# An AdaLN block with a Mamba-2 scan on one core: the first stage moved into the main block, wide modulation products, a polynomial log1p, C stored once

## The chip, the cores and the metric

The kernel runs on one core of a Trainium2 chip. The metric is the device time of one execution in microseconds, the median of several. All data is float32. Matmuls whose operands are typed float32r take one record in the profile, those on plain float32 take two.

## What is computed

The reference, cut to what matters here (4 batches of 512 tokens, width 512; 64 value heads of 16, 8 groups of 64 states, chunks of 64 in this kernel):

```python
mod = (silu(c) @ wmod).reshape(4, 6, 1, -1)           # (4,512) @ (512,3072)
sa, ca, ga, sb, cb, gb = (mod[:, i] for i in range(6))
h = layernorm(x) * (1 + ca) + sa
xBCzA = einsum('bld,ed->ble', h, in_proj_w)           # x 1024, B 512, C 512, z 1024, A_log 64
xBC = silu(conv1d(xBC, taps=4) + bias)
dt = softplus(A_log)                                  # log1p(exp(-|a|)) + max(a, 0)
y = ssd_chunk_scan(x, -dt, B, C) + D * x / dt         # per head
x = x + ga * ((y * silu(z + z_bias)) @ out_proj_w.T)
h = layernorm(x) * (1 + cb) + sb
x = x + gb * (h @ binarize(ffn_w).T + bias)
```

The scan per group and chunk: G = B C^T (gram); M = G times exp of differences of summed dt (mix); y = M x (diagonal) + exp(sums) * C S (offdiagonal); S = decay * S + B^T (w x) (fade, states, update).

## The kernel before

There are three parts: `prologue`, a block of its own that ends in a barrier over all engines; `main_part`; and `tail_part` (output projection and second half), which the change touches only in the names of PSUM banks.

`prologue` makes, in this order on each engine: the modulation (`section(0)` and `section(1)`: transposed products with 4 columns, 16 matmuls a section); statistics and normalisation of the 16 x tiles, their transposition (`turn`), `h_hi` and `h_lo` (`make_h`, `low_part`), four tiles of 128x512 a batch; `dt_inputs` for the two pairs of batches (`pb` 0 and 1), 24 matmuls each; two more sections; the weights of the first six tiles (`weights`); the two gate sections in the wide form (4x512 outputs). Meanwhile DVE computes dt for both pairs, interleaved: log1p by a series of atanh (21 operations a pair, two reciprocals among them), the summed dt, their ends, low parts, skips D/dt. All goes to scratch in DRAM; the main block reads it back, among it the negated sums (`na_scratch`).

`main_part` works in 16 steps (4 group pairs by 4 batches), each with 4 units of 128 tokens; 64 units in all, each of four slots. A fixed table (`tile_order`) says which half projection (6 matmuls of 512 columns) stands in which slot, a lag table when its linear part, taps, tanh and silu follow. The first four tiles (x, x, B, C of step 0) are projected ahead of the loop. In unit v's slot 0 PE runs `offdiagonal(v)` (L1039), `states(v+1)` (L1052), `diagonal(v)` (L1065), `gram(v+1)` (L1077); `turn_x` (L1019), `turn_b` (L1029) and `decay` (L1010) of unit v+2 stand in slots 1 to 3. DVE runs `update`, `collect` and `mix` (L1277) in slots 1 and 2, convolutions (L1241) and silus (L1263, L1268) between. C is stored as a block diagonal of two 64-row halves, the rest zero, so that full 128-row matmuls give both groups at once.

## Time and profile before

| | |
|---|---|
| median of 3 runs | 749.23 us (749.15 to 751.7) |
| profiled execution | 748.24 us |
| its span, first to last instruction | 746.5 us |
| mean granted PE clock | 0.944 of full speed |
| PE, DVE, ACT, POOL busy | 674.1, 536.5, 376.5, 389.4 us |

A row of the timeline reads: start, duration, engine, line, operation, output <- inputs, shape, count; in brackets the idle time before it and what ended it. Ends of matmuls are modelled, so the distance between starts is what counts on PE.

### The profile page before, as it was taken

The numbers are of one execution on the slowest core, as the hardware profiler recorded it, in microseconds if no ns is written. First come the engines' busy times: TensorE is split into PE (matmuls) and PEld (weight loads), VectorE is DVE, ScalarE is ACT, GpSimd is POOL, SyncE is SP. The second block draws the span as 40 slices with busy tenths as digits, with TensorE's granted clock in tenths as the row PEclk, the third lists the DMA queues.
The fourth block names the chain that finished last, engine by engine and source line by source line (L and its number), as shares of the span: only waits on it lengthen the run. The fifth ranks groups of instructions, "written<-read, shape, count | busy, mean of one in ns | idle before, by whom it ended". The sixth has DMA issues, their size and how long they took to land. (4 is left out here: it accounts for less than half of the span.)

```text
span 746.5 us, 20781 instructions
## 1 busy us (share of the span) xinstructions
PE 674.1 (90%) x8194; PEld 527.1 (71%) x8194; DVE 536.5 (72%) x940; ACT 376.5 (50%) x812; POOL 389.4 (52%) x465
## 2 busy tenths in 40 slices
PE   6679256899999999999999999999998999999995
PEld 6458115677777777787777777777776777777783
DVE  2768675878788688778777777877779567576754
ACT  1563241444564554465454456555665534555453
POOL 3674920125365454375363365454645767677771
PEclk9757577999999999999999999999999999999997
DMA  8450262103132112222212225223212664443401
GB/s 207 107 177 12 80 247 90 32 16 110 37 104 84 58 61 72 82 92 61 92 58 69 70 80 152 91 68 114 77 48 70 202 191 134 141 136 112 128 28 43
DMA packets 61908, 71.54 MB, mean 96 GB/s; under 512 B 13992, under 2 KB 32936, under 8 KB 61812
## 3 DMA queue, kind: packets, MB, share of 16 engines
q1 hardware_dynamic: 56372, 70.17, 29.6%
q8 instruction: 65, 1.06, 0.6%
q10 hardware_dynamic: 5440, 0.05, 0.4%
q14 instruction: 31, 0.25, 0.1%
HBM read 54.45 MB, written 15.75 MB: 94 GB/s over the span
## 5 line engine op out<-in xcount | busy, mean ns | idle before, releaser
L1241 DVE SCALAR_TENSOR_TENSOR m_cv<-bank,gpc,m_cv 128x511 f32<-128x511 f32 (+2 forms) x192 | 143.5, 748 | 44.9 <-ACT m_cv L1151 40.3
L1001 PE MATMUL bank<-h_hi,w_hi 128*128 128x512 f32 x384 | 159.0, 414 | 12.8 <-DVE m_Xp L1323 11.5
L1001 PE MATMUL bank<-h_hi,w_lo 128*128 128x512 f32 x384 | 151.8, 395 | 0.0
L1001 PE MATMUL bank<-h_lo,w_hi 128*128 128x512 f32 x384 | 151.5, 394 | 0.0
L1151 ACT ACTIVATE m_cv<-bank,gpc 128x512 f32<-128x512 f32 x96 | 71.9, 748 | 92.0 <-PE bank L1001 92.0
L1379 POOL TENSOR_TENSOR m_S<-m_S,m_cd 128x128 f32<-128x128 f32 x96 | 39.7, 414 | 141.0 <-DVE m_S L1304 71.4
L1001 PEld LDWEIGHTS bank<-h_hi,w_hi 128*128 128x128 f32 x384 | 73.0, 190 | 31.9 <-DVE m_Xp L1323 11.7
L1370 POOL TENSOR_TENSOR m_Xw<-m_Xp,wend 128x256 f32<-128x256 f32 x64 | 39.8, 622 | 105.8 <-ACT m_Xp L1171 105.8
L1001 PEld LDWEIGHTS bank<-h_hi,w_lo 128*128 128x128 f32 x384 | 72.6, 189 | 17.1
L1001 PEld LDWEIGHTS bank<-h_lo,w_hi 128*128 128x128 f32 x384 | 73.1, 190 | 13.7
L1163 ACT ACTIVATE m_M<-bank 128x512 f32<-128x512 f32 x128 | 76.2, 595 | 12.0 <-PE bank L1010 10.5
L1277 DVE TENSOR_TENSOR m_M<-m_M,bank 128x512 f32<-128x512 f32 x128 | 81.7, 679 | 0.0
L1065 PE MATMUL pair<-m_M,m_Xp 64*32 64x64 f32 x4096 | 61.6, 227 | 0.0
L1010 PE MATMUL bank<-R,Lm 84*128 84x512 f32 x128 | 57.2, 447 | 3.2 <-ACT m_M L1163 3.2
L1158 ACT ACTIVATE bank<-m_cv 128x512 f32<-128x512 f32 x96 | 58.2, 606 | 2.6 <-DVE m_cv L1241 2.6
L1707 PE MATMUL bank<-h_hi,t_y_hi 128*128 128x512 f32 x128 | 52.1, 407 | 7.0 <-POOL t_y_lo L1584 7.0
L1065 PEld LDWEIGHTS pair<-m_M,m_Xp 64*32 64x32 f32 x4096 | 54.0, 106 | 1.1
L1584 POOL TENSOR_TENSOR t_y_lo<-h_lo_place,t_y_hi 128x1024 fp32r<-128x1024 f32 x16 | 40.1, 2504 | 27.3 <-ACT t_y_hi L1545 27.3
L1707 PE MATMUL bank<-h_hi,t_y_lo 128*128 128x512 f32 x128 | 50.7, 396 | 0.0
L1707 PE MATMUL bank<-h_lo,t_y_hi 128*128 128x512 f32 x128 | 50.7, 396 | 0.0
L1268 DVE SCALAR_TENSOR_TENSOR m_gate<-bank,m_cv 128x512 f32<-128x512 f32 x32 | 22.1, 691 | 39.3 <-ACT bank L1158 39.3
L1171 ACT ACTIVATE m_Xp<-bank 128x256 f32<-128x256 f32 x64 | 24.2, 379 | 49.0 <-PE bank L1019 49.0
(183 smaller groups left out, 1376.3 us busy)
## 6 DMA issues: line engine op xcount, KB each, us to landing
m_ea<-ea_scratch SPq DMA_DIRECT2D x32, 256.0 KB
m_dd<-dd_scratch SPq DMA_DIRECT2D x32, 256.0 KB
y_scratch<-m_t SPq DMA_DIRECT2D x16, 512.0 KB, 3.4
h_lo_place<-y_scratch SPq DMA_DIRECT2D x16, 512.0 KB, 4.3
p_wm<-in_L_wmod_dram SPq DMA_DIRECT2D x6, 1024.0 KB, 6.4
m_wraw<-in_L_attn_in_proj_w_dram SPq DMA_DIRECT2D x18, 256.0 KB, 2.9
p_xt<-in_L_attn_input__dram SPq DMA_DIRECT2D x16, 256.0 KB, 3.0
w_lo_place<-in_L_attn_input__dram SPq DMA_DIRECT2D x16, 256.0 KB, 4.5
```

The source lines that it names most:

```text
L1001: ins = pe.matmul(A[k % 3][:, :], w[:, t, kc, :], h[:, n % NB, kc, :], start=(m == 0), stop=(m == 11))
L1010: pe.matmul(DB[:, :], s.Lm[:, u % 2, q, :], s.R[:, u % 2, q, :], start=True, stop=True).then_inc(d_done, 1)
L1065: ins = pe.matmul(YS[32 * j:32 * j + 32, c, q * Q:(q + 1) * Q], Xp[half, u % 2, HG * q + h, :], M[half, u % 2, q, h * Q:(h + 1) * Q], star ...
L1151: act.activation(cv[:, k % 3, :], A[k % 3][:, :], ACT.Identity, scale=scale, bias=bias).then_inc(lin_done, 1)
L1158: act.activation(A[k % 3][:, :], cv[:, k % 3, :], ACT.Tanh).then_inc(tanh_done, 1)
L1163: act.activation(M[:, u % 2, q, :], DB[:, :], ACT.Exp).then_inc(exp_done, 1)
L1241: ins = dve.scalar_tensor_tensor(out=cv[:, k % 3, lag:], in0=A[k % 3][:, 0:L - lag], scalar=s.gpc[:, gp, o:o + 1], in1=cv[:, k % 3, lag:], ...
L1277: dve.tensor_tensor(m, m, g, ALU.mult).then_inc(m_done, 1)
L1370: pool.tensor_tensor(Xw[:, :, :].rearrange("p q (j e d) -> p (q j) e d", e=2, d=HD), src, w, ALU.mult).then_inc(xw_done, 1)
L1379: pool.tensor_tensor(S1[:, c, :].rearrange("p (h d) -> p h d", h=HG), S[:, (m - 1) % 4, :].rearrange("p (h d) -> p h d", h=HG), cd[:, gp, ...
L1584: pool.tensor_tensor(y_lo[:, st.b % 2, :, :], yt_v(st.b), y_hi[:, st.b % 2, :, :].bitcast(F32), ALU.subtract).then_inc(ylo_done, 1)
L1707: ins = pe.matmul(OB[i][:, :], y[:, i, k, :], w[k], start=(k == 0 and m == 0), stop=(k == KI - 1 and m == 2))
```

## The change

The prologue is no longer a block of its own: `first_part` defines functions that the main block's engines call ahead of their loops, so the barrier goes. The x tiles are loaded before the modulation weights. All six sections are wide products (4 matmuls with 512 columns), copied to SBUF and turned back by four small transposes. dt of batches 0 and 1 (`pb` 0) is computed early; x tiles 12 to 15, the projections of the first four tiles, and the inputs of dt of batches 2 and 3 follow. Of `pb` 1, `softplus` and `finish_times` stand ahead of DVE's loop, `sums`, `low_sums` and `skips` inside it (units -1, 1, 3), the decays on ACT in unit 1, the turn of the end decays in unit 4, their copies in unit 5; the stores and the chunk decays of `pb` 1 in SP's units 2 and 5. log1p is a polynomial of degree 11. The negated copies in scratch are gone (the constant is -1 instead). C is stored once, `[P, 2, L]`, and `offdiagonal`, `states` and `gram` use 64x64 tiles; gram's product moves to PSUM beside the others (`YS[:, q, 384:448]`), which brings waits on `g_done` for `collect` and `update`, and `offdiagonal` waits for `m_done` in place of `turn_b`.

```diff
+LOG1P = [1.0, -0.5, 0.33333237, -0.2499676, 0.19956708, -0.16365153, 0.13033364, -0.09139414, 0.04930997, -0.01718427,
+         0.00280164]
...
-            for k in (15, 13, 11, 9, 7, 5, 3):
-                for pb in range(2):
-                    r, e, den, sv, tt, pl, dt, tmp = half_of(pb)
-                    linked(pb)
-                    link(pb, dve.scalar_tensor_tensor(out=pl, in0=pl, scalar=1.0 / k, in1=tt, op0=ALU.add, op1=ALU.mult))
...
+        sp.dma_start(c4[:, :], cond).then_inc(d_c, 16)
+        for i in range(4):
+            load_x(i)
+        sp.dma_start(wa_raw[:, :], w_in[2 * DI + 2 * NG * NS:, :]).then_inc(d_wa, 16)
+        load_section(0)
+        load_section(1)
+        for i in range(4, 8):
+            load_x(i)
+        load_weights(0)
+        load_weights(1)
+        for i in range(8, 12):
+            load_x(i)
+        load_weights(2)
+        load_weights(3)
+        load_section(2)
+        load_section(3)
+        for i in range(12, 16):
+            load_x(i)
+        load_weights(4)
+        load_weights(5)
+        load_section(4)
+        load_section(5)
...
+        normalize(10)
+        normalize(11)
+        softplus(dve, 0)
+        finish_times(dve, 0)
+        sums(dve, 0)
+        skips(dve, 0)
+        low_sums(dve, 0)
...
+        normalize(15)
+        low_part(9)
+        low_part(11)
+        convolve(0)
+        convolve(1)
+        silu(0)
+        low_part(13)
+        low_part(15)
+        convolve(2)
+        silu(1)
+        convolve(3)
+        silu(2)
+        silu(3)
+        modulation(2)
+        modulation(3)
+        gates()
+        softplus(dve, 1)
+        finish_times(dve, 1)
...
+    def softplus(dve, pb):
+        e, pl = s.chain[:, pb, 1, :], s.chain[:, pb, 3, :]
+        dve.wait_ge(a_exp[pb], 3)
+        dve.tensor_scalar(pl, e, LOG1P[-1], None, ALU.mult).then_inc(a_v[pb], 1)
+        for i, c in enumerate(LOG1P[-2:4:-1]):
+            chained(dve, pb, 1 + i)
+            dve.scalar_tensor_tensor(out=pl, in0=pl, scalar=c, in1=e, op0=ALU.add, op1=ALU.mult).then_inc(a_v[pb], 1)
+    def finish_times(dve, pb):
+        dt, e, pl = (s.chain[:, pb, i, :] for i in (0, 1, 3))
+        for i, c in enumerate(LOG1P[4::-1]):
+            chained(dve, pb, 6 + i)
+            dve.scalar_tensor_tensor(out=pl, in0=pl, scalar=c, in1=e, op0=ALU.add, op1=ALU.mult).then_inc(a_v[pb], 1)
+        chained(dve, pb, 11)
+        dve.tensor_tensor(dt, pl, dt, ALU.add).then_inc(a_v[pb], 1)
+        chained(dve, pb, 12)
+        dve.tensor_scalar(e, dt, DT_MAX, -1.0, ALU.min, ALU.mult).then_inc(a_v[pb], 1)
+    def sums(dve, pb):
+        end, pl = s.chain[:, pb, 1, :], s.chain[:, pb, 3, :]
+        plv = pl.rearrange("p (c q) -> p c q", q=Q)
+        dve.wait_ge(konst, 16)
+        chained(dve, pb, A_DT)
+        dve.tensor_tensor_scan(out=pl, data0=chunk_on[:, :], data1=end, initial=0.0,
+                               op0=ALU.mult, op1=ALU.add).then_inc(a_v[pb], 1)
+        chained(dve, pb, A_SUM)
+        dve.tensor_tensor(end.rearrange("p (c q) -> p c q", q=Q), plv[:, :, Q - 1:Q].broadcast_to([P, NC, Q]), plv,
+                          ALU.subtract).then_inc(a_v[pb], 1)
+    def low_sums(dve, pb):
+        hi, pl = s.chain[:, pb, 2, :], s.chain[:, pb, 3, :]
+        dve.wait_ge(a_act[pb], B_CD)
+        dve.tensor_tensor(pl, pl, hi, ALU.subtract).then_inc(a_v[pb], 1)
+    def skips(dve, pb):
+        dt = s.chain[:, pb, 0, :]
+        dve.reciprocal(dt, dt).then_inc(a_skip, 1)
+        dve.wait_ge(a_skip, 2 * pb + 1)
+        dve.tensor_scalar(dt, dt, dcol[:, 0:1], None, ALU.mult).then_inc(a_skip, 1)
...
+    def decays(act, pb):
+        end, hi, pl, ea = (s.chain[:, pb, i, :] for i in (1, 2, 3, 4))
+        act.wait_ge(a_v[pb], A_END)
+        act.activation(hi.bitcast(F32R), pl, ACT.Copy).then_inc(a_act[pb], 1)
+        act.activation(ea, pl, ACT.Exp).then_inc(a_act[pb], 1)
+        act.activation(cde[:, pb, :], pl.rearrange("p (c q) -> p c q", q=Q)[:, :, Q - 1], ACT.Exp).then_inc(a_act[pb], 1)
+        act.activation(end, end, ACT.Exp).then_inc(a_act[pb], 1)
...
-                for m in range(KC):
-                    for k in range(KC):
-                        ins = pe.matmul(MOD[n // 2][:, (n * KC + m) * NB:(n * KC + m + 1) * NB],
-                                        wm[:, n % 2, k, m * P:(m + 1) * P], scT[:, k, :],
-                                        start=(k == 0), stop=(k == KC - 1))
-                ins.then_inc(mod_pe, 1)
...
+            for k in range(KC):
+                ins = pe.matmul(row_bank(n)[0:NB, :], scT[:, k, :], wm[:, n % 2, k, :], start=(k == 0), stop=(k == KC - 1))
+            ins.then_inc(sec_pe, 1)
...
+        def turn_section(n):
+            pe.wait_ge(sec_cp, n + 1)
+            for k in range(KC):
+                ins = pe.transpose(mod_bank(n)[:, k * NB:(k + 1) * NB], row_of(n)[:, k * P:(k + 1) * P], s.ident[0:NB, 0:NB])
+            ins.then_inc(mod_pe, 1)
...
+        for i in range(4, 8):
+            turn(i)
+        for n in range(4):
+            weights(n)
+        pe.wait_ge(wa_dve, 1)
+        dt_inputs(0)
+        pe.wait_ge(w_act, 4)
+        for i in range(8, 12):
+            turn(i)
+        for n in range(4, 8):
+            weights(n)
+        project(0, 0)
+        project(0, 1)
+        section(2)
+        section(3)
+        project(1, 0)
+        project(1, 1)
+        turn_section(2)
+        turn_section(3)
+        for i in range(12, 16):
+            turn(i)
+        project(2, 0)
+        project(2, 1)
+        for n in range(8, 12):
+            weights(n)
+        project(3, 0)
+        project(3, 1)
+        section(4)
+        section(5)
+        pe.wait_ge(w_act, 12)
+        end_turn(pe, 0)
+        turn_section(4)
+        turn_section(5)
+        dt_inputs(1)
+        pe.wait_ge(gate_v, 3)
+        pe.transpose(MOD[0:2 * NB * KC, 0:P], ga[:, :, :, :].rearrange("p g b k -> p (g b k)"), s.ident[:, :]).then_inc(gate_pe, 1)
+        pe.wait_ge(gate_ready, 1)
+        pe.wait_ge(a_exp[1], 2)
...
+                if v == -1:
+                    start.store_skips(sp, 0)
+                    for i2 in range(2):
+                        sp.wait_ge(start.h_lo[i2], 8)
+                    load_skips(0)
+                if v == 2:
+                    start.store_decays(sp, 1)
+                    load_chunk_decays(1)
+                if v == 5:
+                    start.store_skips(sp, 1)
+                if v == 4 or (v > 2 and i == 2 and n < LAST):
+                    load_skips(v // UPS + (v != 4))
...
-                wait(pe, m_done, 2 * u)
                 wait(pe, bt_read, u)
-                pe.transpose(GB[:, P:2 * P], Bt[:, n % 2, tok(u)], s.ident[:, :]).then_inc(bt_done, 1)
+                pe.transpose(GB[:, 0:P], Bt[:, n % 2, tok(u)], s.ident[:, :]).then_inc(bt_done, 1)
             def offdiagonal(u):
                 n = u // UPS
                 wait(pe, y1_done, u)
                 pe.wait_ge(s_new, n_new(u, 1))
+                pe.wait_ge(m_done, 2 * u + 2)
...
-                    ins = pe.matmul(YS[:, c, P:2 * P], S[:, (2 * u + c - 1) % 4, :], Ct[:, n % 2, :, chunk(u, c)],
-                                    start=True, stop=True)
+                    for j in range(2):
+                        for q in range(2):
+                            group, strip = slice(64 * q, 64 * q + 64), slice(64 * j, 64 * j + 64)
+                            ins = pe.matmul(YS[strip, q, P + Q * c:P + Q * c + Q], S[group, (2 * u + c - 1) % 4, strip],
+                                            Ct[group, n % 2, chunk(u, c)], start=True, stop=True)
...
-                for m in range(4):
+                for q in range(2):
                     for c in range(2 if u % UPS < UPS - 1 else 1):
-                        half = slice(64 * c, 64 * c + 64)
-                        ins = pe.matmul(YS[32 * m:32 * m + 32, c, 256:384], BTs[half, 32 * m:32 * m + 32], Xw[half, m // 2, :],
-                                        start=True, stop=True)
+                        half, group = slice(64 * c, 64 * c + 64), slice(64 * q, 64 * q + 64)
+                        ins = pe.matmul(YS[group, c, 256:384], BTs[half, group], Xw[half, q, :], start=True, stop=True)
...
-                for m in range(4):
-                    first = (u % UPS) * U_TOK + 32 * m
-                    ins = pe.matmul(GB[32 * m:32 * m + 32, 0:P], Bt[:, n % 2, first:first + 32], Ct[:, n % 2, :, chunk(u, m // 2)],
-                                    start=True, stop=True)
+                for c in range(2):
+                    for q in range(2):
+                        group = slice(64 * q, 64 * q + 64)
+                        ins = pe.matmul(YS[64 * c:64 * c + 64, q, 384:384 + Q], Bt[group, n % 2, chunk(u, c)],
+                                        Ct[group, n % 2, chunk(u, c)], start=True, stop=True)
...
-            pe.wait_ge(zeroed, 1)
-            for k in range(4):
-                project(k, 0)
-                project(k, 1)
+            start.tensor(pe, project)
...
+                    if (v, sl) == (4, 3):
+                        pe.wait_ge(xp_done, u + 1)
+                        start.end_turn(pe, 1)
...
+                    if (v, sl) == (1, 1):
+                        start.decays(act, 1)
+                    if (v, sl) == (5, 0):
+                        start.end_copy(act, 1)
...
-                if t == 3:
-                    for q in range(2):
-                        rows = slice(64 * q, 64 * q + 64)
-                        ins = dve.scalar_tensor_tensor(out=Ct[rows, n % 2, q, :], in0=A[k % 3][rows, :], scalar=1.0,
-                                                       in1=cv[rows, k % 3, :], op0=ALU.add, op1=ALU.mult)
-                    ins.then_inc(silu_done, 1)
-                    return
...
-                g = GB[:, q * Q:(q + 1) * Q].unsqueeze(1).broadcast_to([P, HG, Q])
+                g = YS[:, q, 384:384 + Q].unsqueeze(1).broadcast_to([P, HG, Q])
...
+                dve.wait_ge(g_done, min(u + 2, NU))
...
+                dve.wait_ge(g_done, u + 1)
...
-            dve.memset(Ct[:, :, :, :], 0.0)
-            dve.memset(Xp[:, :, :, :], 0.0).then_inc(zeroed, 1)
-            dve.wait_ge(zeroed, 1)
-            convolve(0)
-            convolve(1)
-            silu(0)
-            convolve(2)
-            silu(1)
-            convolve(3)
-            silu(2)
-            silu(3)
+            start.vector(dve, convolve, silu)
...
+                    if (v, sl) == (-1, 3):
+                        start.sums(dve, 1)
+                    if (v, sl) == (1, 3):
+                        start.low_sums(dve, 1)
+                    if (v, sl) == (3, 3):
+                        start.skips(dve, 1)
```

Where instructions move. First PE in unit 0 of the loop, from the turn of B of unit 2 to the gram of unit 1, before:

```order
L1029 MATMUL bank<-ident,m_Bt 128x128 [waits m_bt_read,m_m_done]
L1039 MATMUL pair<-m_Ct,m_S 128x128 [waits m_s_new]
L1052 MATMUL pair<-m_Xw,m_BTs 32x128 [waits m_bt_read,m_xw_done,m_s_new]
L1052 MATMUL pair<-m_Xw,m_BTs 32x128 x7
L1065 MATMUL pair<-m_M,m_Xp 32x64 [waits m_xp_done,m_m_done]
L1065 MATMUL pair<-m_M,m_Xp 32x64 x31
L1077 MATMUL bank<-m_Ct,m_Bt 32x128 [waits m_bt_read]
L1077 MATMUL bank<-m_Ct,m_Bt 32x128 x3
```

The same place after the change:

```order
L1176 MATMUL bank<-ident,m_Bt 128x128 [waits m_bt_read]
L1190 MATMUL pair<-m_Ct,m_S 64x64 [waits m_m_done,m_s_new]
L1190 MATMUL pair<-m_Ct,m_S 64x64 x3
L1203 MATMUL pair<-m_Xw,m_BTs 64x128 [waits m_bt_read,m_xw_done,m_s_new]
L1203 MATMUL pair<-m_Xw,m_BTs 64x128 x3
L1215 MATMUL pair<-m_M,m_Xp 32x64 [waits m_xp_done,m_m_done]
L1215 MATMUL pair<-m_M,m_Xp 32x64 x31
L1228 MATMUL pair<-m_Ct,m_Bt 64x64 [waits m_bt_read]
L1228 MATMUL pair<-m_Ct,m_Bt 64x64 x3
```

One matmul of 128 columns became four of 64 (two became eight in the other units), eight became four, and the wait on `m_m_done` moved from the turn to the first of them. Second, DVE around the first taps of the loop itself; before, from C's silus of step 0:

```order
L1263 SCALAR_TENSOR_TENSOR m_Ct<-bank,m_cv 64x512 [waits m_tanh_done]
L1263 SCALAR_TENSOR_TENSOR m_Ct<-bank,m_cv 64x512
L1241 SCALAR_TENSOR_TENSOR m_cv<-bank,gpc,m_cv 128x511 [waits m_lin_done]
L1241 SCALAR_TENSOR_TENSOR m_cv<-bank,gpc,m_cv 128x510 [waits m_tap_done]
L1241 SCALAR_TENSOR_TENSOR m_cv<-bank,gpc,m_cv 128x509 [waits m_tap_done]
L1304 COPY m_S<-pair 128x128 [waits m_st_done]
```

After, from C's one silu of step 0 (`chain` holds dt and its sums):

```order
L1414 SCALAR_TENSOR_TENSOR m_Ct<-bank,m_cv 128x512 [waits m_tanh_done]
L461 TENSOR_SCALAR mod_t<-pair 128x16 [waits p_mod_pe] x2
L482 TENSOR_SCALAR p_gs<-pair 128x32 [waits p_gate_abs]
L483 TENSOR_SCALAR p_ga<-p_ga 128x32
L485 SCALAR_TENSOR_TENSOR p_ga<-p_gs,p_ga 128x32 [waits p_gate_v]
L559 TENSOR_SCALAR chain<-chain 128x512 [waits p_a_exp1]
L562 SCALAR_TENSOR_TENSOR chain<-chain 128x512 [waits p_a_v1] x5
L569 SCALAR_TENSOR_TENSOR chain<-chain 128x512 [waits p_a_v1] x5
L571 TENSOR_TENSOR chain<-chain 128x512 [waits p_a_v1]
L573 TENSOR_SCALAR chain<-chain 128x512 [waits p_a_v1]
L1393 SCALAR_TENSOR_TENSOR m_cv<-bank,gpc,m_cv 128x511 [waits m_lin_done]
```

The gates and the second pair's dt now stand between the first four tiles and the loop's first taps.

## Rows read from the trace of the kernel before

**Rows 1.** The page: busy time, and the clock in 40 slices (tenths).

```profile
PE 674.1 (90%) x8194; PEld 527.1 (71%) x8194; DVE 536.5 (72%) x940; ACT 376.5 (50%) x812; POOL 389.4 (52%) x465
...
PEclk9757577999999999999999999999999999999997
```

**Rows 2.** Timeline, 0 to 50 us: modulation products, statistics, h, dt inputs.

```profile
6.78 13.79 PE L653 MATMUL pair<-p_scT,p_wm 128*128 128x4 f32 x64 [2.36 <-DMA p_wm<-in_L_wmod_dram]
7.37 0.69 DVE L408 BATCH_NORM_STATS2 p_st<-p_xt 128x6 f32<-128x512 f32 x1 [2.73 <-DMA p_xt<-in_L_attn_input__dram]
...
25.39 0.78 ACT L575 ACTIVATE h_hi<-bank,mod_t 128x512 fp32r<-128x512 f32 x1 [3.72 <-PE bank L670]
...
30.04 0.81 ACT L579 ACTIVATE p_hf<-bank,mod_t 128x512 f32<-128x512 f32 x1
...
33.41 0.78 ACT L575 ACTIVATE h_hi<-bank,mod_t 128x512 fp32r<-128x512 f32 x1 [2.56 <-PE pair L670]
...
49.19 0.78 PE L684 MATMUL bank<-h_hi,p_wa_hi 128*128 128x512 f32 x1
```

**Rows 3.** Timeline, 54 to 100 us: the dt series, GpSimd beside it, wide sections.

```profile
56.54 0.69 DVE L466 TENSOR_SCALAR p_a<-bank 128x512 f32<-128x512 f32 x1 [0.52 <-PE bank L684]
...
73.11 11.12 POOL L378 TENSOR_TENSOR w_lo<-p_wst,w_hi 128x256 fp32r<-128x256 f32 x1 [9.83 <-ACT p_wst L616]
...
74.61 4.90 DVE L488 SCALAR_TENSOR_TENSOR p_a<-p_a 128x512 f32<-128x512 f32 x8
...
82.50 2.81 DVE L506 TENSOR_TENSOR_SCAN p_a<-p_chunk_on,p_a 128x512 f32<-128x512 f32 x2
...
85.24 2.28 DVE L514 TENSOR_TENSOR p_a<-p_a 128x512 f32<-128x512 f32 x2
...
91.17 1.41 POOL L378 TENSOR_TENSOR w_lo<-p_wst,w_hi 128x256 fp32r<-128x256 f32 x2 [0.30 <-ACT p_wst L616]
...
94.97 9.62 PE L728 MATMUL bank<-p_wm,p_scT 128*4 128x512 f32 x16 [1.65 <-DMA p_wm<-in_L_wmod_dram]
...
97.47 3.35 DVE L526 RECIPROCAL p_a<-p_a 128x512 f32<-128x512 f32 x1
```

**Rows 4.** Busy us of PE, PEld, DVE, ACT, POOL in a window; PEclk; DMA share; GB/s.

```profile
75.00:80.00 5.00, 0.00 (x0) 0.00 (x0) 5.00 (x9) 0.00 (x0) 5.00 (x1) 0.50 0.21 52
...
295.00:323.00 28.00, 27.95 (x453) 22.14 (x452) 21.50 (x41) 14.46 (x32) 11.07 (x16) 1.00 0.23 73
```

**Rows 5.** Timeline where the main block begins: first projection, turn_x(0), taps of tile 4.

```profile
117.11 0.80 PE L1001 MATMUL bank<-h_hi,w_hi 128*128 128x512 f32 x1 [11.50 <-DVE m_Xp L1323]
...
132.66 0.38 PE L1019 MATMUL bank<-ident,m_xs 128*128 128x128 f32 x2
...
136.68 2.32 DVE L1241 SCALAR_TENSOR_TENSOR m_cv<-bank,gpc,m_cv 128x511 f32<-128x511 f32 x3
```

**Rows 6.** Timeline of PE, slot 0 of two units of the loop.

```profile
318.32 0.39 PE L1039 MATMUL pair<-m_Ct,m_S 128*128 128x128 f32 x2
318.73 0.45 PE L1052 MATMUL pair<-m_Xw,m_BTs 64*32 64x128 f32 x16
...
325.59 0.61 PE L1039 MATMUL pair<-m_Ct,m_S 128*128 128x128 f32 x4
326.21 0.45 PE L1052 MATMUL pair<-m_Xw,m_BTs 64*32 64x128 f32 x16
326.44 0.91 PE L1065 MATMUL pair<-m_M,m_Xp 64*32 64x64 f32 x64
327.28 0.43 PE L1077 MATMUL bank<-m_Ct,m_Bt 128*32 128x128 f32 x8
327.64 0.44 PE L1094 MATMUL bank<-ident,m_wraw 128*128 128x128 f32 x2
```

**Rows 7.** The last turn_x on PE; then from the waits, 150 to 630 us: total, times, longest.

```profile
593.42 0.38 PE L1019 MATMUL bank<-ident,m_xs 128*128 128x128 f32 x2
...
PEld bank L1029 <- DVE m_M L1277: 2.7, 6, 1.9
```

974 lines of the change are left out of this document (488 added, 486 removed).

## The prediction

> **What bounds the kernel now.** I read the page first, then its 40 slices, then the timeline of the first 140 us, then two units of the main loop. The page [rows 1] shows TensorE (PE) busy for 90% of the span and no other engine over 72%. Its clock row stands under 9 from the second to the seventh slice, up to 131 us, and not again before the last one: there PE runs with gaps and for long stretches at half clock. So there are two regimes, and the change touches both.
>
> In the main loop PE is the bound. In a window of 28 us [rows 4] PE is busy for 27.95 and DVE for 21.50, so DVE has 6.5 us free, about 1.7 us a unit. Unit 0 turns its x at 132.66 [rows 5] and unit 63, the last of 64, at 593.42 [rows 7]: 460.8 us for 63 units, 7.31 us each.
>
> The first stage is a chain over all engines. PE is busy for 0.00 us between 75 and 80 [rows 4] while DVE works through the softplus series. In turn: the modulation products end at 20.57 and the first normalised tile of h is made at 25.39 [rows 2]; h is made batch by batch, the inputs of dt start on PE at 49.19; DVE's chain for all four batches follows, and only then does a barrier let the first projection begin, at 117.11, after 11.50 us in which PE waited for the zeroing of Xp on DVE [rows 5]. The first convolution that belongs to the loop itself (tile 4) starts on DVE at 136.68 [rows 5]. I take that row as the anchor: behind it both kernels have the same list of work on DVE, but for what the change moves there.
>
> **The first stage, step by step.** The changed one is laid out by hand, each engine in its order, with durations of before.
>
> (a) The x tiles are loaded ahead of the wide weights, so statistics can start at about 4.5 instead of 7.37 [rows 2]. The modulation takes 8 records of 512 columns a section instead of 32 of 4 columns. Before, two sections took 13.79 us for 64 records [rows 2]. The gates were already made in the wide form, 16 records in 9.62 us, 0.60 each [rows 3], partly at half clock. At full clock I estimate 0.42 (four times the 0.105 of a 128-column record, below): 3.4 a section. The weights land later, behind 1.1 MB of x; I put section 0 at 9.3, two turns of 0.65 between, section 1 up to 17.4, a copy, four small turns and the additions 2 us: h from 19.5, not 25.39.
>
> (b) A batch of h takes ACT 5.46 us (25.39 to 30.85 [rows 2]). Batches followed each other every 8.0 us (25.39 to 33.41), which DVE and GpSimd set with the statistics: the next one from 28, until 33.5. With its last low part 35, then the dt inputs of batches 0 and 1: 24 matmuls, 7.3 us before (49.19 to the first DVE reader at 56.54 [rows 2, 3]): 43. Three activations: 45.
>
> (c) DVE's chain for these two: the series was 21 operations for each pair of batches, two of them reciprocals of 3.35; now it is 18 with one. A link is 4.90 / 8 = 0.61 with two chains interleaved [rows 3]; alone I take 0.70. 11 x 0.70 + 1.4 (scan) + 1.14 (end) + 3.35 + four lesser ones at 0.5 = 15.6: 61. Meanwhile GpSimd is held up: its low part of the weights took 11.12 us beside DVE's links and 0.70 where DVE was idle [rows 3]. Its four weight pieces, for which ACT waits and with ACT the exponentials of the decays, end about 60: 63 for DVE.
>
> (d) Tiles 12 to 15 are normalised: 75. h of batch 3 on ACT: 81. DVE works off four low parts, twelve taps and four silus meanwhile; PE projections 2 and 3, with weights between: 88.
>
> (e) PE then has in a row sections 4 and 5 (6.9), small turns (1.5) and the dt inputs of batches 2 and 3 (6 to 7): 103; softplus inputs 105. DVE: 11 x 0.70 and two lesser ones, 8.7: 113.7. For stretches at half clock, which bursts after a gap had before, I add 2.4: **the anchor comes at 116, 20.7 us earlier**. PE, which would be ready for unit 0 at 107, 25 earlier, waits for DVE in the first units.
>
> (f) What went into the loop: for batches 2 and 3 scan, ends, low sums and skips, 1.4 + 1.14 + 3.35 and two lesser ones, 7 us on DVE (units -1, 1 and 3), 2.9 us of activations on ACT, four turns on PE. It lies beside 1.7 us a unit of free DVE time, 13 us over eight units; where that cover is gone it costs 7. As the backlog of (e) uses the same cover, I charge **2.0**. SP's queue: the stores of batches 2 and 3 stand behind the loads for units 4 to 6, whose data is wanted two units later; nothing.
>
> **The loop, per unit.** Removed: one of two DVE silus of C in four units, off the bound. On PE [rows 6]: L1039 is 0.41 to the next row with two records and 0.62 with four, so 0.105 a record and 0.20 fixed, the emptying of the array before the next tile shape. L1052, L1065 and L1077 are 0.23, 0.84 and 0.36, that is 13.1 ns a record in L1065; L1077 as two rounds of 0.105 with 0.15 fixed. With L1039's mean (half a unit fewer in four) the three that change cost 1.16 a unit.
>
> After, they are 14, 7 and 8 records on 64x64 tiles, and the order of shapes gives one more change between full and split array. No row has this tile. Lower bound: a record of 64 columns goes at 13.1 ns whatever its width, one of 128 columns in a quarter of 0.105: 0.18 + 0.18 + 0.10, and three emptyings of 0.15 = 0.91, so -0.25 a unit. Upper bound: 13.1 ns is the load of 32 columns and 64 take 26.2: 0.37 + 0.18 + 0.21 and 0.45 = 1.21, +0.05. The rows can't separate them (every split row loads 32 columns). I choose -0.05, nearer the upper one, since 64 columns load twice of what L1065 loads. **62 x -0.05 = -3.**
>
> "TensorE: Matmul & The Clock Gate", section LDWEIGHTS, of the Trainium skill says that a weight load's time goes by the number of columns alone; "TensorEngine Tiling (Array Packing)", Key Properties, of the Trainium skill says that a change of tiling mode drains the array. By both the loop would lose its 0.05 a unit, 3 us, and the time would be 733.
>
> The wait for C's product moves: it is no longer turn_b that waits for M's last product but L1039 one row later, so nothing is added. New is that DVE's update and collect wait for gram, about 0.36 after the diagonal; behind them stands M's product, for which PE waited in about 6 of 62 units, 2.7 us in all [rows 7].
>
> **Sum.** The profiled execution took 748.24, its span 746.5, the median is 749.23. 748.24 - 20.7 + 2.0 - 3.1 = 726.4; with the median's 1 us more, 727.
>
> **Rivals.**
> - *As forecast*, first stage 14 to 27 earlier, loop within 0.1 a unit: 716 to 736. 0.52.
> - *64x64 tiles pay*: -0.25 to -0.35 a unit (the longer if turn_b's missing wait and L1039's fixed part go too), 15 to 22 us and the first stage at its best: 703 to 716. For it: half of C's columns were zeros. 0.22.
> - *Loads by columns, with another emptying of the array*: 0.05 to 0.2 a unit, 3 to 12: 733 to 742. 0.10.
> - *The first stage hardly gains*: GpSimd held up by both series, and PE at half clock in six short bursts (each up to 3.4 more): 8 us earlier instead of 20.7: 740 to 745. 0.07.
> - *Slower*: DVE's round becomes the loop. Update and collect start 0.36 later and the additional emptying adds 0.15, and if M's product is then always late, a unit takes 0.5 more: 31 us, less 20: 757. It decides from 0.4 a unit (25 us). For it: the 6 late products. Against: 6.5 us in 28 free on DVE. 0.06.
> - The rest, under 703: 0.03.
>
> **Numbers.** 727; range 703 to 742 leaves out the last two and part of the fourth. 0.5% is 3.7 us, about what a measurement of this kernel can tell from no change: faster 0.90, same 0.04, slower 0.06.
>
> **What would show it.** First h_hi at 19 to 21; dt inputs at 35; DVE's first chain ending near 63; sections 4 and 5 near 88 to 95; the tile-4 convolution at 112 to 120; the turn of unit 63 about 24 us earlier; spacing of units 7.2 to 7.35; L1190 with four instructions a chunk 0.4 to 0.55 to the next row. I am wrong if the second series holds up PE for over 8 us in units -2 to 2, if the unit's spacing leaves 7.0 to 7.4, or if PE waits for M's product in most units.

## The result, and the profile after

The changed kernel takes **722.11 us** in the median of 4 runs (720.19 to 725.2), the kernel before beside it 749.76: a ratio of **0.9631**, 95% interval 0.9591 to 0.9671, 27 us less. The forecast was 727, the range 703 to 742. The profiled execution of after took 725.2 us, 3 above its median.

From the page of the changed kernel:

```profile
PE 660.5 (91%) x8347; PEld 497.3 (69%) x8347; DVE 516.7 (71%) x913; ACT 379.1 (52%) x818; POOL 374.9 (52%) x464
...
PEclk9678899999999999999999999999999999999995
```

It answers to [rows 1]: TensorE is still the bound, with fewer busy microseconds, and its clock row is back at 9 after the fifth slice (90 us), not after the seventh (131 us). The 9 of the first slice says little: this trace has no clock level for the first 15.07 us, and the views count such time as full. I come back to this at the narrow sections.

The timeline of the first stage, selected rows of PE, ACT and DVE in order of time:

```profile
11.65 5.28 PE L739 MATMUL bank<-p_wm,p_scT 128*4 128x512 f32 x8 [0.19 <-DMA p_wm<-in_L_wmod_dram]
17.89 3.60 PE L739 MATMUL bank<-p_wm,p_scT 128*4 128x512 f32 x8
22.90 0.78 ACT L643 ACTIVATE h_hi<-bank,mod_t 128x512 fp32r<-128x512 f32 x1 [0.79 <-DVE mod_t L461]
48.44 0.43 DVE L559 TENSOR_SCALAR chain<-chain 128x512 f32<-128x512 f32 x1 [0.27 <-ACT chain L655]
48.90 4.54 DVE L562 SCALAR_TENSOR_TENSOR chain<-chain 128x512 f32<-128x512 f32 x5
53.48 6.27 DVE L569 SCALAR_TENSOR_TENSOR chain<-chain 128x512 f32<-128x512 f32 x5
66.69 0.68 DVE L591 TENSOR_TENSOR chain<-chain 128x512 f32<-128x512 f32 x1
87.91 7.03 PE L739 MATMUL bank<-p_wm,p_scT 128*4 128x512 f32 x16
103.84 0.43 DVE L559 TENSOR_SCALAR chain<-chain 128x512 f32<-128x512 f32 x1 [5.35 <-ACT chain L655]
104.71 0.38 PE L1167 MATMUL bank<-ident,m_xs 128*128 128x128 f32 x2
113.00 2.31 DVE L1393 SCALAR_TENSOR_TENSOR m_cv<-bank,gpc,m_cv 128x511 f32<-128x511 f32 x3
117.45 0.80 PE L1158 MATMUL bank<-R,Lm 84*128 84x512 f32 x1 [4.61 <-ACT m_M L1316]
```

The first h starts at 22.90 (25.39 in [rows 2]); the turn of unit 0 on PE at 104.71 (132.66 in [rows 5]), 28.0 earlier; but the taps of tile 4, my anchor, at 113.00 (136.68 in [rows 5]), 23.7 earlier. The last five rows show why: DVE works off the second softplus series from 103.84 to 113.0, the taps stand behind it, ACT's tanh behind the taps, and PE idles 4.61 us.

A second stall, on DVE and PE five units later:

```profile
149.25 3.34 DVE L596 RECIPROCAL chain<-chain 128x512 f32<-128x512 f32 x1
...
157.00 0.47 PE L1149 MATMUL bank<-h_hi,w_hi 128*128 128x512 f32 x1 [1.68 <-DVE m_xs L1414]
```

From one turn of x to the next the first units take 7.1 to 7.2 us (units 0 to 1: 6.15), but 13.54 between units 1 and 2 and 9.21 between 6 and 7. Unit 8 turns at 169.42 (190.84 before), 21.4 earlier; unit 63 at 570.63 (593.42 in [rows 7]), 22.8 earlier. So the whole loop behind unit 8 gave 1.4 us in 55 units.

Two units of the loop on PE (left out: projections, decay products):

```profile
318.43 0.27 PE L1176 MATMUL bank<-ident,m_Bt 128*128 128x128 f32 x1
318.54 0.38 PE L1245 MATMUL bank<-ident,m_wraw 128*128 128x128 f32 x2
318.85 0.46 PE L1190 MATMUL pair<-m_Ct,m_S 64*64 64x64 f32 x16
319.16 0.45 PE L1203 MATMUL pair<-m_Xw,m_BTs 64*64 64x128 f32 x8
319.54 0.86 PE L1215 MATMUL pair<-m_M,m_Xp 64*32 64x64 f32 x64
320.32 0.34 PE L1228 MATMUL pair<-m_Ct,m_Bt 64*64 64x64 f32 x8
320.60 0.44 PE L1245 MATMUL bank<-ident,m_wraw 128*128 128x128 f32 x2
...
325.78 0.28 PE L1176 MATMUL bank<-ident,m_Bt 128*128 128x128 f32 x1
325.99 0.34 PE L1190 MATMUL pair<-m_Ct,m_S 64*64 64x64 f32 x8
326.52 0.45 PE L1203 MATMUL pair<-m_Xw,m_BTs 64*64 64x128 f32 x8 [0.18 <-ACT m_BTs L1329]
```

Read starts, not durations. From the off-diagonal product (L1190) to the states (L1203) it is 0.31 with 16 records and 0.53 with 8. What decides is the row ahead of it, not the count: over 150 to 560 us it is 0.31 behind a piece of weights and 0.53 behind the turn of B, with 8 and with 16 records alike. From the turn of B (L1176) to the states it is 0.73 and 0.74. I come back to this.

### The profile page after: what moved, and what is told of

Same layout as the page of the kernel before. It is cut to its first block and busy times, and to the rows that moved or that the text cites. A ratio compares the mean times of both kernels' runs of the same rounds, so it can differ in the third digit from the quotient of the medians.

```text
span 723.5 us, 21285 instructions
## 1 busy us (share of the span) xinstructions
PE 660.5 (91%) x8347; PEld 497.3 (69%) x8347; DVE 516.7 (71%) x913; ACT 379.1 (52%) x818; POOL 374.9 (52%) x464
## 5 line engine op out<-in xcount | busy, mean ns | idle before, releaser
L1149 PE MATMUL bank<-h_hi,w_hi 128*128 128x512 f32 x384 | 161.0, 419 | 4.8 <-ACT p_hf L647 1.7
L1149 PE MATMUL bank<-h_hi,w_lo 128*128 128x512 f32 x384 | 153.9, 401 | 0.0
L1149 PE MATMUL bank<-h_lo,w_hi 128*128 128x512 f32 x384 | 153.4, 400 | 0.0
L1149 PEld LDWEIGHTS bank<-h_hi,w_hi 128*128 128x128 f32 x384 | 74.4, 194 | 20.7 <-issue 6.8
L1423 DVE TENSOR_TENSOR m_M<-m_M,pair 128x512 f32<-128x512 f32 x128 | 81.7, 678 | 0.2 <-issue 0.2
L1215 PE MATMUL pair<-m_M,m_Xp 64*32 64x64 f32 x4096 | 55.4, 224 | 0.0
L1734 POOL TENSOR_TENSOR t_y_lo<-h_lo_place,t_y_hi 128x1024 fp32r<-128x1024 f32 x16 | 39.6, 2474 | 27.8 <-ACT t_y_hi L1695 27.8
L1215 PEld LDWEIGHTS pair<-m_M,m_Xp 64*32 64x32 f32 x4096 | 45.0, 105 | 10.9 <-issue 10.9
```

What stands on the lines that cost most here:

```text
L1149: ins = pe.matmul(A[k % 3][:, :], w[:, t, kc, :], h[:, n % NB, kc, :], start=(m == 0), stop=(m == 11))
L1215: ins = pe.matmul(YS[32 * j:32 * j + 32, c, q * Q:(q + 1) * Q], Xp[half, u % 2, HG * q + h, :], M[half, u % 2, q, h * Q:(h + 1) * Q], star ...
L1423: dve.tensor_tensor(m, m, g, ALU.mult).then_inc(m_done, 1)
L1734: pool.tensor_tensor(y_lo[:, st.b % 2, :, :], yt_v(st.b), y_hi[:, st.b % 2, :, :].bitcast(F32), ALU.subtract).then_inc(ylo_done, 1)
```

## The experiments

The changed kernel came out at 0.9631 and, in a second measurement, at 0.9663 of the kernel before; 0.965 is the yardstick below, and a thousandth is 0.75 us. Single traces of one and the same kernel differ by up to 3.4 us in when the first stage ends, so within a trace I read distances.

**The form of C alone.** The kernel before, with offdiagonal, states, gram, the silu of C and their waits as in the changed one:

```
-                    ins = pe.matmul(YS[:, c, P:2 * P], S[:, ...], Ct[:, n % 2, :, chunk(u, c)], ...)
+                    for j in range(2):
+                        for q in range(2):
+                            ins = pe.matmul(YS[strip, q, ...], S[group, ..., strip], Ct[group, n % 2, chunk(u, c)], ...)
```

> The kernel before, with only the form of C changed: C kept once, its products on 64x64 tiles, states on 64x64 tiles, gram written beside them, the waits that go with it. The zeroing of C's storage stays, so the first stage is untouched. My reading of the trace after (14 + 7 + 8 records cost 1.98 us a unit against 2.05 before, loop spacing 0.025 shorter) gives 62 x -0.025 = -1.6 us: ratio 0.996 to 1.000. If 64x64 tiles paid as the rival had it (-0.25 a unit), 733 to 735, ratio 0.98. If loads by columns and another emptying decided (+0.05), 752, ratio 1.004.

Measured: 746.16 us (12 runs) beside 747.72, ratio 0.9993 (0.9972 to 1.0014); a unit takes 7.234 us (mean of units 12 to 43) where 7.268 was. From the turn of unit 0 to that of unit 63 the two traces differ by 2.0 us (458.8 in place of 460.8), as much as I had expected; in the time the interval reaches from 2 us less to 1 us more. The form of C is worth nothing that the time can show; the rival "64x64 tiles pay" and the one that had them cost 3 to 12 us both fall.

**Gram first.** One group moved:

```
                             states(v + 1)
+                            gram(v + 1)
                         if v >= 0:
                             diagonal(v)
-                        if 0 <= v + 1 < NU:
-                            gram(v + 1)
```

> The changed kernel, with gram issued between states and diagonal: the three products on 64x64 tiles then follow one another and a unit has one change of tile shape fewer (3 in place of 4). If each change costs an emptying of about 0.15 us, and the small products save nothing because of them, a unit takes 0.10 to 0.15 less, 6 to 9 us over 62 units: ratio to the changed kernel 0.988 to 0.992, ratio to the kernel before 0.951 to 0.956. If the change of shape costs nothing and the loads of 64 columns are what eats the gain, nothing: 722, ratio to before 0.963. If DVE's round were close to the bound, gram earlier gives M's product an earlier start and a gain too, but then PE's waits would go and not the spacing of rows in the group.

Measured: 714.47 us, ratio 0.9545 (0.9522 to 0.9568), 8 us less than the changed kernel. The rows of gram_first for the same place in the loop:

```profile
315.67 0.45 PE L1203 MATMUL pair<-m_Xw,m_BTs 64*64 64x128 f32 x8
315.91 0.32 PE L1228 MATMUL pair<-m_Ct,m_Bt 64*64 64x64 f32 x8
316.17 0.86 PE L1215 MATMUL pair<-m_M,m_Xp 64*32 64x64 f32 x64
316.95 0.44 PE L1245 MATMUL bank<-ident,m_wraw 128*128 128x128 f32 x2
```

States and gram took 0.38 + 0.28 = 0.66 us to their next rows; now 0.24 + 0.26 = 0.50. Same records, same shapes, one change from 64x64 to 64x32 tiles and back less: 0.16 us. A unit takes 7.101 in place of 7.256, 0.155 less, and waits of PE are as before. So a change of shape is the price, not the load of 64 columns. What gram's move would give with the old form of C was not tested.

**The second series spread over the loop.** Its 13 links are issued by a table of places behind the taps, the sums a unit or two later:

```
+SERIES_AT = {(-2, 3): 2, (-1, 0): 1, (-1, 1): 1, (-1, 2): 1, (-1, 3): 2, (0, 1): 1, (0, 3): 2, (1, 1): 3}
-        softplus(dve, 1)
-        finish_times(dve, 1)
```

> The changed kernel, with the second softplus series (13 links, 9.2 us on DVE) taken out from ahead of the loop and spread over units -2 to 1 behind the taps, sums, low sums, the decays on ACT and their stores one unit or two later. If the 4.6 us wait of PE in unit 0 (turn to turn 13.54 us where 7.2 is usual) is that series standing ahead of tile 4's taps, the turn of unit 2 comes 4 to 6 us earlier against the first h, and the time falls by 3 to 5: 717 to 719, ratio to before 0.956 to 0.960. If DVE has not 1.7 us a unit free there, the stall only moves to later units and the time stays within 1 us of 722.

Measured: 721.91 us, ratio 0.9647 (0.9621 to 0.9673): nothing that can be told. The wait of 4.61 is gone (unit 2 follows unit 1 by 7.19), but unit 3 takes 11.06, unit 5 8.39, unit 7 9.18, and units 0 to 8 take 64.2 us where they took 64.7. Windows of series_spread (columns: busy time of each engine, then PE's clock):

```profile
core 0: us, PE busy (x) PEld busy (x) DVE busy (x) ACT busy (x) POOL busy (x), PEclk, DMA share, GB/s
103.00:110.00 7.00, 6.54 (x43) 5.16 (x44) 2.60 (x5) 3.31 (x7) 0.62 (x1) 1.00 0.02 5
110.00:117.00 7.00, 6.82 (x112) 5.13 (x111) 6.49 (x12) 3.33 (x7) 1.71 (x3) 1.00 0.13 44
117.00:124.00 7.00, 4.30 (x21) 3.22 (x20) 6.86 (x15) 3.26 (x6) 1.40 (x3) 1.00 0.44 152
```

From 110 to 124 DVE is busy for 6.5 and 6.9 of 7 us; in the changed kernel, without the series in the loop, it is 6.9 from 120 to 127 and 6.1 in the next window. My "1.7 us a unit of free DVE time" is true of a unit in the middle of the loop [rows 4], not of the first ones. The stall is DVE's list, wherever its parts stand. What is free is DVE's time ahead of the loop's work: it is busy for 2.60 of 7 us in the first window.

**The last reciprocal in four pieces.**

```
+SKIP_AT = {(2, 3): 0, (3, 1): 1, (3, 3): 2, (4, 1): 3}
+        dt = s.chain[:, 1, 0, i * P:(i + 1) * P]
+        dve.reciprocal(dt, dt).then_inc(a_skip, 1)
```

> The changed kernel, with the reciprocal of 512 columns of the second skips (3.34 us on DVE in unit 3) cut into four of 128 columns in units 2 to 4. If that one long instruction is what PE waits 1.68 us for in unit 5 (spacing 9.21 in place of 7.2), the spacing there falls to 7.2 to 7.4 and the time by 1.8 to 2.1: 720, ratio to before 0.960. If DVE is simply full in these units, the wait stays wherever the work is put: 722.

Measured: 721.57 us, ratio 0.9642 (0.962 to 0.9664). The stall is gone in the trace (unit 7 follows unit 6 by 7.26, units 0 to 8 take 62.9 in place of 64.7), 1.8 us; the total can't tell 1.8 us from nothing. Here the length of one instruction was the cause and not the sum of the work.

**The changed kernel again.**

> The changed kernel unaltered, as the yardstick for the others on this chip: ratio to before 0.961 to 0.966, first turn at 103 to 105, unit 2 at 13.3 to 13.7 us behind unit 1, unit 7 at 9.2 behind unit 6.

Measured: ratio 0.9663 (0.9639 to 0.9687); spacings 13.85 and 9.19. Its first turn came at 101.33, 3.4 earlier than in the trace above. Its first loads had landed earlier (first h at 21.35, 1.6 earlier); the rest arose on the way.

**The dt inputs of batches 2 and 3 first.** On PE ahead of sections 4 and 5, with ACT and DVE to match:

```
+        dt_inputs(1)
         section(4)
         section(5)
...
-        dt_inputs(1)
```

> The changed kernel, with the dt inputs of batches 2 and 3 on PE ahead of the wide sections 4 and 5 (which only the gates need), the last tanh and the softplus inputs ahead of their copies on ACT, and DVE's second series begun before the gates' additions and finished behind them. The work is the same. In the changed kernel DVE idles 5.1 us before C's silu and 5.35 us before the second series, then PE idles 4.61 us for it; in series_spread the stall moved into later units because DVE was busy 6.8 of 7 us there. If that is the cause, the series put into DVE's earlier idle time takes the stall away for good: taps of tile 4 at 106 to 108 in place of 113.0, unit 2 within 8 us of unit 1, time 4 to 5.5 us less than the unaltered one: 715 to 717, ratio to before 0.956 to 0.958. If the stall is DVE's backlog of the loop itself (taps and silus of tiles 4 to 6), at most 1 us is won.

Measured: 716.31 us, ratio 0.9571 (0.9551 to 0.9591), some 6 us less. DVE in dt_first:

```profile
93.64 0.43 DVE L559 TENSOR_SCALAR chain<-chain 128x512 f32<-128x512 f32 x1 [2.73 <-ACT chain L655]
...
100.94 3.60 DVE L569 SCALAR_TENSOR_TENSOR chain<-chain 128x512 f32<-128x512 f32 x5
...
107.66 2.32 DVE L1393 SCALAR_TENSOR_TENSOR m_cv<-bank,gpc,m_cv 128x511 f32<-128x511 f32 x3 [1.64 <-ACT m_cv L1304]
```

The series starts 10 us earlier, in idle time, and the taps 5.3 us earlier, now with DVE waiting for them; unit 2 follows unit 1 by 7.18. With series_spread this shows the cause of the first stall: work of DVE left for the loop's beginning that had room before it.

**Statistics and small loads early.** The twelve small loads go from ACT's queue to the sync queue, DVE's statistics of tiles 4 to 6 ahead of the modulation's additions.

```
+        statistics(dve, 4)
+        statistics(dve, 5)
+        normalize(4)
+        statistics(dve, 6)
+        normalize(5)
         modulation(0)
         modulation(1)
```

> The changed kernel, with the twelve small vector loads on the sync queue behind the first weights in place of ahead of ACT's copy of the dt weights, and DVE's statistics of x tiles 4 to 6 ahead of the modulation's additions. In the changed kernel ACT idles 15.9 us while these loads are issued, DVE idles 7.06 behind it, and batch 1 of h starts at 32.59 where ACT had finished batch 0 at 28.4. If DVE's late start is what sets batch 1, it starts at 28.5 to 29.5, the first series ends 3 to 4 us earlier (63 in place of 66.7), and the first turn comes 2 to 4 us earlier; time 718 to 720. The first h_hi itself should stay at 22.5 to 22.9, since PE's second section (ends at 21.49) sets it. If PE's own list from the first projection on (sections, projections, turns) sets the end of the first stage, nothing of it is left at the first turn.

Measured: 720.32 us, ratio 0.9617 (0.96 to 0.9634). ACT and DVE no longer idle where they did, but batch 1 of h comes only 0.9 us earlier behind batch 0:

```profile
22.56 1.26 POOL L403 TENSOR_TENSOR h_lo<-p_hf,h_hi 128x512 fp32r<-128x512 f32 x1 [4.45 <-ACT p_hf L647]
23.79 0.22 POOL L411 TENSOR_SCALAR p_rstd<-p_mv 128x1 f32<-128x1 f32 x1
...
29.82 0.78 ACT L643 ACTIVATE h_hi<-bank,mod_t 128x512 fp32r<-128x512 f32 x1 [3.32 <-PE bank L758]
```

The root of tile 6 (23.79) stands in GpSimd's order behind low part 0, which waits for ACT. From the first h to the scan of the first series it is 37.2 us, where it is 37.9 to 38.2 in five traces with this stretch unaltered and 39.3 in two more. A fault of my edit, mended in the last kernel; what it gives by itself lies between 1 and 3 us.

**The polynomial alone**, in the kernel before:

```
-                    link(pb, dve.reciprocal(tmp, den))
+            for c in LOG1P[-2::-1]:
+                    link(pb, dve.scalar_tensor_tensor(out=pl, in0=pl, scalar=c, in1=e, op0=ALU.add, op1=ALU.mult))
```

> The kernel before, with only the softplus series changed: the polynomial in place of the series with a quotient, for both pairs of batches. 28 operations of which two reciprocals of 3.35 us become 24 without one, 7.8 us less on DVE in the stretch in which PE is idle. If DVE's series is on the path to the first projection, the first turn comes 7 to 8 us earlier and the time is 740 (ratio 0.989 to 0.991), so over a quarter of the first stage's gain is the polynomial's and the rest the order's. If GpSimd's low parts or the loads end last there, 0 to 3 us.

Measured: 745.03 us, ratio 0.9949 (0.9936 to 0.9963), about half of what I expected; first turn 2.1 us earlier. Three rows of poly_alone say where it went:

```profile
62.70 0.69 DVE L468 TENSOR_SCALAR p_a<-bank 128x512 f32<-128x512 f32 x1 [3.15 <-PE bank L667]
...
92.99 9.54 PE L711 MATMUL bank<-p_wm,p_scT 128*4 128x512 f32 x16 [3.40 <-DMA p_wm<-in_L_wmod_dram]
...
115.08 0.80 PE L984 MATMUL bank<-h_hi,w_hi 128*128 128x512 f32 x1 [11.51 <-DVE m_Xp L1306]
```

The first reciprocal had lain beside PE's second dt inputs, for which DVE now waits 3.15 us, so the scan comes 3.5 us earlier (82.50 in [rows 3]) and not 7.8; then the gates' weights arrive late, and the first projection is 2.0 earlier (117.11 in [rows 5]).

**The first projections last.** Four projections, their activations, taps and silus stand behind the whole first stage, as behind the barrier before:

```
         pe.wait_ge(a_exp[1], 2)
+        for k in range(4):
+            project(k, 0)
+            project(k, 1)
```

> The changed kernel, with the overlap of the first projections undone: projections 0 to 3, their activations, taps and silus stand behind the whole first stage (behind the second series on DVE), as the barrier had them in the kernel before; everything else, the order of the rest included, is as changed. If the gain came from PE and DVE working beside the first stage, the work put back behind it is 4 projections on PE (2.8 us each) and 12 taps and 4 silus on DVE (about 12 us): the first turn comes 11 to 13 us later, but DVE's series starts up to 10 us earlier, so the taps of tile 4 come 4 to 10 us later than 113.0 and the time is 726 to 732, ratio to before 0.969 to 0.977; most of the 28 us would then be the order within the first stage. If the overlap is the whole gain, 740 and more.

Measured: 735.11 us, ratio 0.9815 (0.9794 to 0.9836), 12 us more than the changed kernel. In the trace:

```profile
100.46 0.43 DVE L559 TENSOR_SCALAR chain<-chain 128x512 f32<-128x512 f32 x1 [6.68 <-ACT chain L655]
...
114.53 0.77 PE L1144 MATMUL bank<-h_hi,w_hi 128*128 128x512 f32 x1 [6.23 <-DVE m_xs L1409]
```

The second series starts only 3.4 us earlier than with the projections between: they had filled gaps (DVE is busy for 20.8 of the 45 us from 56 to 101, against 31.2 of 48 in the changed kernel). I had put that at up to 10, hence 735 and not 726 to 732. The overlap of the first projections is a little under half of the gain, 12 of 27 us. The first turn came 16.5 us later (121.17 against 104.71), where I had expected 11 to 13.

**The first two sections narrow**, 32 records of 4 columns as before:

```
+                wm_steps = [(mod_bank(n)[...], wm[:, n % 2, k, j * P:(j + 1) * P], k) for j in range(KC) for k in range(KC)]
-        turn_section(0)
-        turn_section(1)
```

> The changed kernel, with sections 0 and 1 of the modulation (the two that the first h waits for) in the form of before: 32 records of 4 columns with the weights as the loaded side, no copy and no small turns for them; sections 2 to 5 stay wide. Before, two sections took 13.79 us for 64 records; the wide ones took 4.85 and 3.60 and two copies with turns about 1.5 more. If the wide form is worth the difference, the first h starts 4 to 5 us later (26 to 28 in place of 21.4 to 22.9) and the time rises by as much: 725 to 728, ratio 0.969 to 0.972. If the weights' arrival (8.5 us a section) sets the sections' pace anyway, 0 to 2 us.

Measured: 726.32 us, ratio 0.971 (0.9683 to 0.9737), 4.5 us more. PE and ACT:

```profile
10.93 6.99 PE L739 MATMUL pair<-p_scT,p_wm 128*128 128x4 f32 x32 [0.55 <-DMA p_wm<-in_L_wmod_dram]
19.53 6.83 PE L739 MATMUL pair<-p_scT,p_wm 128*128 128x4 f32 x32
26.68 0.78 ACT L643 ACTIVATE h_hi<-bank,mod_t 128x512 fp32r<-128x512 f32 x1 [9.46 <-DVE mod_t L461]
```

h waits for both sections, so their length counts in full. But it is not the number of records that makes them shorter. Windows of the kernel before, in its second pair of narrow sections (columns as above; the number behind `x` counts records):

```profile
62.00:66.00 4.00, 4.00 (x39) 4.00 (x37) 2.64 (x4) 3.01 (x5) 1.15 (x3) 1.00 0.02 4
67.00:71.00 4.00, 4.00 (x20) 4.00 (x21) 4.00 (x8) 0.00 (x0) 0.00 (x0) 0.50 0.00 0
```

At full clock 39 records of 4 columns fit into 4 us, at half clock 20: 0.11 and 0.213 us each, so a narrow section of 32 takes 3.5 or 6.8 us. A wide one takes 8 x 0.43 = 3.4 at full clock, and its records are 0.85 apart at half clock (below), which makes 6.8. At the same clock the two forms cost the same. The narrow sections here took 6.99 and 6.83, and the 64 records of before 13.79 [rows 2]: 0.213 each, half clock. What differs is when the clock rises. The first clock level in a trace is a full one and starts at 12.2 to 15.2 us in the ten traces with wide first sections, and at 24.7 to 53.7 in the four with narrow ones, this one included. Here it starts at 48.5, and the dt inputs' records follow each other by 0.43 us up to there and by 0.23 from there on. By these distances the 4.5 us are the clock's and not the form's. PE had been busy for 15.4 of the 15.5 us from 10.9 to 26.4 with the narrow records; why the clock stayed low beside them no run tells.

**Combined**: the changed kernel with gram first, dt inputs first, the reciprocal in pieces, the early statistics, and GpSimd's roots 6 and 7 ahead of its low parts:

```
         root(5)
+        root(6)
+        root(7)
         low_part(0)
-        root(6)
         low_part(2)
```

> The changed kernel with what paid: gram between states and diagonal (9 us), the dt inputs of batches 2 and 3 ahead of sections 4 and 5 (5.5 to 7), the last reciprocal in four pieces (2), and the small loads and the statistics early, this time with GpSimd's roots of tiles 6 and 7 ahead of its low parts, which stood in their way (in early_stats h of batch 1 waited 3.3 us, where 4.2 had been, for tile 6, whose root stood behind low part 0). If the four add up: 749 - 27 - 9 - 6 - 2 - 3 = 702, ratio 0.937 to 0.943. If DVE's backlog in the first eight units is a common bound, dt_first, skips_split and the early statistics do not add up, and the ratio is 0.945 to 0.950.

Measured: **706.56 us**, ratio **0.9435** (0.9415 to 0.9455), the fastest here, just above the 0.937 to 0.943 that I had expected if all added up. From the turn of unit 0 to that of unit 63 it is 450.3 us in place of 465.9, 15.6 less. In the single traces gram took 8.3 off that distance, the dt inputs 4.6 off that of units 0 to 8, the reciprocal 1.8: 14.7. In the loop they add up. The early statistics gave less than 3: from the first h to the scan it is 37.0 us.

**GpSimd held back**, in the combined kernel:

```
+        pool.wait_ge(a_v[0], A_SUM)
         for n in range(4, 8):
             weights(n)
```

> The combined kernel, with GpSimd's low parts of weight pieces 4 to 7 held until the scan of the first series is done. In the combined kernel the ten links of the first series take 4.54 + 6.29 us (0.91 and 1.26 each) and in the second series 3.60 + 3.59 (0.72 each); the slow ones lie beside GpSimd's low parts (52.71 to 56.86). If it is GpSimd's work beside them that slows the links, the second five fall to 3.6 to 3.8 us and the scan starts 2.5 us earlier against the start of the series; the first five stay at 4.5 (two low parts of h remain beside them). If the links are slow for another reason (the activations beside them, PE at half clock), they stay at 6.3. The time itself: ACT's weight pieces 6 and 7 and with them the first projection are held up to 4 us on PE, so it is 0 to 4 us longer, ratio to before 0.943 to 0.949; if DVE's chain alone set the end of the first stage it would be 2.5 us shorter, 0.940.

Measured: 710.14 us, ratio 0.9508 (0.9484 to 0.9532): by the ratios 5.5 us longer than the combined kernel, by the medians 3.6, at or beyond the upper end of the 0 to 4 that I had expected. In the traces the first turn comes 3.3 us later (104.44 against 101.13), with PE waiting for the weights; another 2.9 us lie in the last five units, which the edit doesn't touch, and their cause is open. What it was made for shows in the view of one line. Columns: shortest, median and longest of ten links, five of each series. First the changed kernel, then gpsimd_waits:

```profile
L569 DVE SCALAR_TENSOR_TENSOR chain<-chain x10: 692/898/1640, 53.5 to 111.2; 128x512 f32<-128x512 f32 x10
```

```profile
L585 DVE SCALAR_TENSOR_TENSOR chain<-chain x10: 684/693/1639, 51.1 to 104.1; 128x512 f32<-128x512 f32 x10
```

The second five of the first series fall from 6.29 in the combined kernel to 4.55 us. What is left over 3.60 is one link of 1.64, beside a low part of h (50.82 to 52.21) that stayed. The first five stay at 4.54, with the other low part of h beside them. The slow links are those beside GpSimd's work.

## Why the prediction held, point by point

**(a) Sections and first h: 19.5 forecast, 22.90 and 21.35 measured.** Two terms failed. Section 0 was to start at 9.3 and started at 11.65, since its weights landed later: 2.35 us. It was to take 3.4, which I had written for full clock, and took 5.28: its first records are 0.81 to 0.85 us apart, which is half clock (below), while section 1 with the same 8 records took 3.60. The steps behind gave back 0.8. That the wide form pays was right in size (narrow_sections: 4.5 us) and wrong in its reason: I compared records of before that ran at half clock with wide ones at full clock, and took the difference for one of the form.

**(b), (c) dt inputs and first series: 35 and 63 forecast, 39.6 and 67.3 measured.** 3.4 of it is (a). The chain itself was put at 15.6 and took 18.9 (48.44 to 67.3). I had foreseen GpSimd's pieces beside it but with the wrong effect: the two engines held each other up by turns, and DVE's links lost 3.6 us in all (10.8 for ten, at 0.72 each 7.2). gpsimd_waits shows it for 1.7 of them; that the rest has the same cause is read from where the slow links lie (below).

**(d), (e) tile 15 normalised at 75, projections done at 88, dt inputs at 103, anchor at 116: 73.7, 87.9, 101.6 and 113.0 measured.** The late start was made up: from the end of the first series to tile 15 I had put 12 us, and it took 6.4 (67.3 to 73.7); the 2.4 for half clock was not needed either (from 86.8 us to the anchor the clock is full). These gains outweigh what (a) and (c) had lost; that the anchor came within 3 us of the forecast is partly luck. The anchor came 23.7 us earlier, forecast 20.7. That PE would be ready and wait for DVE was right (ready at 104.7, idle 4.61 us), and dt_first shows the reason.

**(f) 7 us of DVE work in the loop, charged 2.0: 2.3 measured** (23.7 at the anchor, 21.4 at unit 8), and skips_split finds 1.8 of it in one reciprocal. The size was right by luck: I took it from free time in the middle of the loop, which the first units don't have.

**The loop: -0.05 a unit forecast, -0.025 measured** (1.4 us in 55 units), in the range, with the wrong anatomy. I read L1039's 0.41 and 0.62 us [rows 6] as 0.105 a record with 0.20 for emptying the array. But where the turn of B stands just ahead, that distance is 0.62 with two records too. Behind it is a chain: turn of B on PE, copy on ACT, states on PE. From the turn of B to the states the median is 0.73 us in the changed kernel, with a piece of weights between (23 units) and without (25); before it is 0.73 without, and 0.87 where a piece stands between. The off-diagonal product lies in the shadow of that chain, so its cheaper form shows in a few units only. Means to the next row for states, diagonal and gram: before 0.213, 0.872, 0.357 us, after 0.388, 0.792, 0.276. The last two gave 0.16, and the change of shape behind the states took 0.175.

By rival: the forecast case came in. "Tiles pay" fails on the chain and the change of shape; "loads by columns" on gram, whose 8 records with 64 loaded columns cost 0.26 with a change of shape in it, where my upper bound had 0.21 + 0.15 = 0.36. The slower rival (whose own sum gives 748 + 31 - 20 = 759, not 757) fails too: DVE's round did not become the loop, since PE's waits for M's last product from 180 to 560 us are 1.2 us in all.

**The sum**: -23.7 + 2.3 - 1.4 = -22.8 between the two profiled executions, whose spans differ by 23.0 (746.5 and 723.5); forecast were -21.8. The medians differ by 27.65: the profiled execution of after lies 3.1 above its median and that of before 1.5 below. The other trace of the changed kernel has its first turn 3.4 us earlier, so the 3 may lie in the first stage; that isn't shown.

What gave the 27 us: overlap of the first projections 12, wide sections 4.5, by the clock that rises with them; polynomial about 4 where it stood before; the form of C nothing measurable. The rest, some 6, I can only put down to the remaining order and the lost barrier with its memsets; it was not isolated, and the parts need not add up, since each was taken out of another whole.

## What to carry to other kernels

Where an engine switches tile shapes, put the products of one shape side by side: the new form of C was worth nothing measurable until gram moved beside the others, and then 8 us. Before you compare two forms of a product, bring them to the same clock: read it from the distance between equal records, above all where the trace has no clock level. Before you cheapen an operation, read the distance from the start of the wait it stands in: one that lies in the shadow of a turn, copy and use chain has no price. Free time of an engine is that of its own stretch: DVE had 1.7 us a unit in mid-loop, none in the first units, and 5 us ahead of them.
